# A transformer stack on one core: fp32 score products, another fill of the expert rows, other due times, and a place column for each tile

## The reference, cut to what matters

```python
# L0 xattn: causal-masked linear attention over the context; here Q is norm(x), K is ctx
x = x + _L0_xattn_ref(_layernorm(x), ctx)
# L0 ffn: inside it 16-head attention (head width 8) and 8 experts, top 2
...
scores = einsum('bhqd,bhkd->bhqk', q, k) / sqrt(8)      # q, k after rotary embedding
scores = where(causal, scores, -inf)
attn = softmax(scores)
x = x + (attn @ v) @ w_up
y_e = (silu(t @ w1[e]) * (t @ w3[e])) @ w2[e]            # 8 experts, width 512, the 2 best of a token
# L1 xattn: 16 heads of 64, queries from x, keys and values from the context
out = softmax(q @ k.T / 8) @ v @ w_out + b_out
# L1 ffn: 16 experts of width 256, the 2 best of a token, plus one shared expert of width 512
```

## Time and profile before

| what | us |
|---|---|
| median of 3 runs | 980.52 |
| lowest and highest run | 978.5, 985.04 |
| profiled execution, its own time | 989.18 |
| its span, first to last instruction | 987.4 |

### The profile page before, as it was taken

One profiled execution on the slowest core, in us unless ns is written; L12 is line 12 of the kernel. 1 busy time (PEld: TensorE's weight loads), 2 busy tenths in 40 slices (PEclk: granted clock), 3 DMA queues, 4 the chain that ended last, 5 costly groups with the idle time before them and its releaser, 6 DMA issues.

```text
span 987.4 us, 24585 instructions
## 1 busy us (share of the span) xinstructions
PE 910.0 (92%) x8304; PEld 813.8 (82%) x8304; DVE 723.1 (73%) x1957; ACT 611.7 (62%) x1694; POOL 293.6 (30%) x375
## 2 busy tenths in 40 slices
PE   4899889887999999998799999999998999898997
PEld 3776666654999999997699888998987988898896
DVE  5768788776676667674889978977876637776757
ACT  3487767773666666675577657786775236665640
POOL 3855666763000000001642435311212003232320
PEclk9899999998999999999799999999999999999999
DMA  8549999201131111113110132030028813232235
GB/s 293 160 161 300 352 245 253 56 29 55 53 137 55 49 51 53 55 34 117 43 35 12 33 98 76 23 98 23 23 65 352 290 44 87 77 90 85 82 114 190
DMA packets 59563, 109.82 MB, mean 111 GB/s; under 512 B 6225, under 2 KB 46033, under 8 KB 58033
## 3 DMA queue, kind: packets, MB, share of 16 engines
q1 hardware_dynamic: 52576, 89.42, 29.6%
q0 software_dynamic: 6864, 18.85, 5.7%
HBM read 62.24 MB, written 46.00 MB: 110 GB/s over the span
## 4 chain that ended last, share of the span: by engine, by line
PE 61%; issue 13%; DVE 9%; DMA 8%; POOL 5%; ACT 2%; SPq 0%; DVEq 0%; POOLq 0%; ACTq 0%
PE ps L888 15%; PE ps L718 8%; PE ps L720 8%; PE ps L719 8%; POOL yt_dram L1962 4%; PE ps L975 3%; DMA xs_dram<-zero 3%; PE ps L985 3%; PE ps L999 3%; PE ps L1057 2%; DMA kv_dram<-BIG 2%; PE ps L786 1%; PE ps L824 1%; PE ps L810 1%; ACT BIG L1151 1%
## 5 line engine op out<-in xcount | busy, mean ns | idle before, releaser
L718 PE MATMUL ps<-BIGR 128*128 128x256 f32 (+1 forms) x826 | 260.5, 315 | 6.5 <-DVE BIGR L1797 2.2
L888 PE MATMUL ps<-BIG 128*128 128x128 f32 x2000 | 253.8, 276 | 11.3 <-DVE BIG L1683 10.2
L888 PEld LDWEIGHTS ps<-BIG 128*128 128x128 f32 x2000 | 238.0, 192 | 15.4 <-DVE BIG L1683 13.1
L720 PE MATMUL ps<-BIGR 128*128 128x256 f32 x778 | 222.3, 286 | 0.0
L719 PE MATMUL ps<-BIGR 128*128 128x256 f32 (+1 forms) x602 | 179.2, 298 | 0.0
L718 PEld LDWEIGHTS ps<-BIGR 128*128 128x128 f32 x826 | 159.3, 193 | 14.4 <-issue 7.5
L720 PEld LDWEIGHTS ps<-BIGR 128*128 128x128 f32 x778 | 148.6, 191 | 0.7
L1197 ACT COPY BIG<-BIG 128x512 f32 (+1 forms) x86 | 70.1, 815 | 100.8 <-PE ps L888 87.2
L719 PEld LDWEIGHTS ps<-BIGR 128*128 128x128 f32 x602 | 116.3, 193 | 2.1 <-issue 0.3
L1676 DVE TENSOR_TENSOR BIGR<-BIG,BIGR 128x512 fp32r<-128x512 f32 (+1 forms) x86 | 80.3, 934 | 34.5 <-ACT BIGR L1206 34.3
L1954 POOL DMA_INDIRECT BIG<-ys_dram,YI x32 | 32.5, 1016 | 232.5 <-DMA ys_dram<-BIG 224.3
(11 more groups left out here) (234 smaller groups left out, 1916.5 us busy)
## 6 DMA issues: line engine op xcount, KB each, us to landing
xs_dram<-zero SPq DMA_DIRECT2D x17, 1024.0 KB, 19.5
BIG<-in_wgu SPq DMA_DIRECT2D x2, 6144.0 KB, 19.1
BIG<-in_wd SPq DMA_DIRECT2D x2, 4096.0 KB, 22.1
BIG<-xs_dram SPq DMA_DIRECT2D x47, 129.5 KB
BIG<-xs_dram SPq DMA_DIRECT2D x39, 128.0 KB
ys_dram<-BIG SPq DMA_DIRECT2D x39, 128.0 KB, 1.7
BIG<-in_wkv SPq DMA_DIRECT2D x2, 2048.0 KB, 9.9
kv_dram<-BIG SPq DMA_DIRECT2D x16, 256.0 KB, 4.1
```

The source lines that it names most:

```text
L718: pe.matmul(o, l[0], r[0], start=start, stop=False)
L720: return pe.matmul(o, l[1], r[0], start=False, stop=stop)
L888: i = pe.matmul(o[:, c * 128:(c + 1) * 128], wt[:, at:at + 128], x[:, k * 128:(k + 1) * 128], start=k == 0, stop=k == 1)
```

## The change

The scores of the first stage are computed from unrounded operands, in one product of fp32 for each row group and query half: queries 0 to 63 with all 128 keys of four heads (512 columns), queries 64 to 127 with keys 0 to 63 (256 columns) and with keys 64 to 127 (256 columns). The mask comes last and signals the banks. `qkl` and `kml` are gone. The rows of the first experts have a tensor of their own, `xs0_dram`, of 256 columns. It is filled by 16 DMAs in eight groups of two; each takes 1088 numbers in a run from every fourth partition of the context tile, so what fills the rows is context and not zeros (what is computed from a row that no token takes is never gathered). `IX` has a column for each tile, and `ix` no longer waits for a scatter. Waits on the loads of the first experts' rows in `pad_sp` and `sc` are gone. `LEAD` has other values.

```diff
-BLANK = [range(2 * g, 2 * g + 2) for g in range(7)] + [range(14, 17)]
+BLANK = [range(2 * g, 2 * g + 2) for g in range(8)]
 LEAD = {
-    "EC": -100, "ET": -200, "K": 100, "K_e": -700, "PV": -100, "Q_e": 200, "SD": 400, "V": 100, "V_e": -100,
-    "W": 100, "ah": -300, "al": -200, "btg": 1800, "c_e": -1700, "ch": 900, "cl": -700, "cnt": -100, "cpow": 1000,
-    "ctxh": -800, "ctxl": -1600, "ep1": -4200, "epow": -1400, "exp0": 200, "exp1": 300, "ga0": 4300,
-    "gates_a": -2300, "hnT": -300, "kmh": -100, "kvwl": -100, "kw": 600, "log": -100, "max3": -100, "nl": 200,
-    "ow": -300, "owl": 1200, "pT3": 100, "pT_e0": 400, "pow2": -1000, "pow3": 200, "pro1": 400, "pro2": -900,
-    "pv": -100, "qkT": -200, "qkv": -300, "qw": -200, "r": 100, "rope": -300, "rope_p": -100, "route1": 2400,
-    "sc1": 1100, "stats1": 800, "swh": 500, "swl": 600, "vw": 1100, "wx": 200, "xbt": 1300, "xf": -300, "xh": 700,
-    "xl": -3000, "xr": 1400
+    "EL": -200, "ET": -200, "K": 100, "K_e": -600, "PV": -300, "Q_e": 200, "SD": 400, "SG": 200, "V": 100,
+    "V_e": -200, "W": 100, "ah": -300, "al": -200, "btg": 2900, "c_e": -1600, "ch": 900, "cnt": -100, "cpow": 900,
+    "eps3": -300, "exp1": 200, "exp2": -200, "ga0": 4500, "gates_a": -6000, "hnT": -100, "hnT_e": -100, "kmh": -1200,
+    "kv_e": -600, "kvwl": -7500, "kwl": 800, "load_kv": 3200, "load_q": 2800, "max3": -300, "nl": 200, "owl": 1100,
+    "pT0": -100, "pT2": -500, "pT3": 100, "pT_e0": 200, "pT_e1": -100, "pT_e2": 100, "pow1": -3300, "pow2": -4500,
+    "pow3": 100, "pro1": 400, "pro2": -2800, "qkT": -600, "qkh": -100, "qkv": -1200, "qw": -700, "ra0": 200,
+    "ra1": -300, "rope": -400, "rope_p": -200, "sc0": 1600, "sc1": 1200, "sm": -800, "ss": 1600, "stats1": 300,
+    "swh": 300, "swl": 500, "tt": -2100, "vw": 1700, "wup": -300, "wx": 200, "xadd": -200, "xbt": 900, "xf": -200,
+    "xh": 1500, "xl": -1600, "xr": 600
 }
...
-        p.add("SP", 120, ("blank", g), ("tt", g - 1) if g else ("kmh", 0), late=4000)
+        p.add("SP", 120, ("blank", g), ("tt", 2 * g - 4) if g >= 2 else ("kmh", 2 * g), late=3000)
...
-        add("DVE", 340, ("qkl", b), ("qkh", b))
...
-        add("POOL", 1250, ("kml", b), ("qkl", b), ("s", b - 2))
-        add("PE", 1200, ("s", b), ("kmh", b), ("kml", b), banks=[("s", (f"exp{g}", b)) for g in range(4)])
+        add("PE", 1350, ("s", b), ("kmh", b), banks=[("s", (f"exp{g}", b)) for g in range(4)])
...
-            add("DVE", 100, "ix", ("xs", r, j), ("ys", r, j - 4), *([("te",)] if j == 0 else []))
+            add("DVE", 100, "ix", ("xs", r, j), *([("te",)] if j == 0 else []))
...
-                q, k = (qkh_[b % 2], qkl_[b % 2]), (kmh_[b % 2], kml_[b % 2])
-                for x, y in ((0, 0), (0, 1), (1, 0)):
-                    if y:
-                        causal(b)
-                        pe.wait_ge(*done("kml", b))
+                q, k = qkt_[b % 2], km_[b % 2].rearrange("p (n t) -> p n t", n=4)
+                for half, keys, masked_too in ((0, slice(0, 128), True), (1, slice(0, 64), False), (1, slice(64, 128), True)):
                     for g in range(4):
-                        at = slice(32 * g, 32 * g + 32)
-                        i = pe.matmul(ps("s", b, i=g)[:, :], q[x][at, 0:128], k[y][at, :], start=x + y == 0, stop=x == 1)
-                        if x == 1:
-                            i.then_inc(*fills("s", b, i=g))
+                        at, rows = slice(32 * g, 32 * g + 32), slice(64 * half, 64 * half + 64)
+                        o = ps("s", b, i=g)[rows, :].rearrange("p (n t) -> p n t", n=4)
+                        pe.matmul(o[:, :, keys], q[at, rows], k[at, :, keys], start=True, stop=not masked_too)
+                causal(b)
...
+                    for rows in range(2):
+                        last[rows].then_inc(*fills("s", b, i=2 * (rows ^ 1) + n))
...
-                if j >= 4:
-                    v.wait_ge(sem(f"results_placed{(j - 4) % 3}"), 16 * stores_before(1, j - 4))
...
             def blank(g):
 
-                if g:
-                    sp.wait_ge(*done("tt", g - 1))
-                    if g >= 3:
-                        sp.wait_ge(sem(f"cleared{g % 3}"), 16 * sum(len(BLANK[k]) for k in range(g % 3, g, 3)))
+                if g == 0:
+                    sp.wait_ge(sem("ct_loaded1"), 16 * (NB // 2 - 2 - len(EARLY_KV)))
+                    sp.wait_ge(sem("ct_loaded2"), 16 * len(EARLY_KV))
+                    sp.wait_ge(*done("kmh", 0))
+                elif g == 1:
+                    sp.wait_ge(*done("kmh", 2))
                 else:
-                    sp.wait_ge(*done("kmh", 0))
-                    sp.wait_ge(sem("zeroed"), 1)
+                    sp.wait_ge(*done("tt", 2 * g - 4))
+                if g >= 3:
+                    sp.wait_ge(sem(f"cleared{g % 3}"), 16 * sum(len(BLANK[k]) for k in range(g % 3, g, 3)))
                 for c in BLANK[g]:
-                    sp.dma_start(XS[0:E0 * CAP, 0:D].rearrange("(e c) n -> c e n", c=CAP)[128 * c:128 * c + 128],
-                                 zero[:, 0:D].rearrange("p (o n) -> p o n", o=1).broadcast_to([128, E0, D])
+                    n = CAP // 16 * D // 32
+                    sp.dma_start(XS0.rearrange("r n -> (r n)").rearrange("(e s k n) -> s k e n", e=E0, s=16, k=32)[c],
+                                 CT[c % 4:128:4, :, :, :].rearrange("p b k t -> p (b k t)")[:, 0:n]
+                                 .rearrange("p (o n) -> p o n", o=1).broadcast_to([32, E0, n])
                                  ).then_inc(sem(f"cleared{g % 3}"), 16)
```

More of the change, by code:

```diff
@@ L502, in program @@
         freed = [sem(f"freed{i}") for i in range(8)]
+        XS0 = nc.dram_tensor("xs0_dram", [E0 * CAP, D], F32, kind="Internal").ap()
         XS = nc.dram_tensor("xs_dram", [E1 * CAP, ROW], F32, kind="Internal").ap()
@@ L598, in program @@
         lat = Space((104, 116))
-        qkh_ = lat.ring(2, 256, r=True)
-        qkl_ = lat.ring(2, 256, r=True)
-        kmh_ = lat.ring(2, 512, r=True)
-        kml_ = lat.ring(2, 512, r=True)
+        qkt_ = lat.ring(2, 256)
+        km_ = lat.ring(2, 512)
         lat = Space((96, 104), (116, 152))
@@ L795, in causal @@
                 for n in range(2):
+                    last = [None, None]
                     for half in range(2):
@@ L801, in causal @@
                             o = ps("s", b, i=g)[64 * half:64 * half + 64, :].rearrange("p (n t) -> p n t", n=4)[:, :, lo:128]
-                            pe.matmul(o, identb[at, at], m.broadcast_to([64, 4, 128 - lo]), start=False, stop=False)
+                            last[rows] = pe.matmul(o, identb[at, at], m.broadcast_to([64, 4, 128 - lo]), start=False, stop=True)
+                    for rows in range(2):
+                        last[rows].then_inc(*fills("s", b, i=2 * (rows ^ 1) + n))
             def pT(b, g):
@@ L1141, in qkh @@
                     act.wait_ge(*full("s", b - 2, i=3))
-                act.copy(qkh_[b % 2], ps("qkT", b)[:, 0:256]).then_inc(S["qk_hi"], 1)
+                act.copy(qkt_[b % 2], ps("qkT", b)[:, 0:256]).then_inc(*frees("qkT", b))
             def exp(b, g):
@@ L1631, in ix @@
                 then()
-                v.scalar_tensor_tensor(out=IX[:, j % 4:j % 4 + 1], in0=xs[:, D + 2:ROW], scalar=128.0 * j,
+                v.scalar_tensor_tensor(out=IX[:, j:j + 1], in0=xs[:, D + 2:ROW], scalar=128.0 * j,
                                        in1=PL[:, j % 4:j % 4 + 1], op0=ALU.mult,
@@ L1904, in kmh @@
             def kmh(b):
-                pool.wait_ge(*done("qkh", b))
+                pool.wait_ge(*emptied("qkT", b))
                 if b >= 2:
                     pool.wait_ge(*full("s", b - 2, i=3))
-                masked(pool, kmh_[b % 2], qkh_[b % 2][:, 128:256]).then_inc(S["keys_masked_hi"], 1)
+                masked(pool, km_[b % 2], qkt_[b % 2][:, 128:256]).then_inc(S["keys_masked"], 1)
             def kvwl(u):
@@ L1915, in kvwl @@
                                    ALU.subtract).then_inc(S["early_w_lo"], 1)
-            def kml(b):
-                pool.wait_ge(*emptied("qkT", b))
-                if b >= 2:
-                    pool.wait_ge(*full("s", b - 2, i=3))
-                masked(pool, kml_[b % 2], qkl_[b % 2][:, 128:256]).then_inc(S["keys_masked_lo"], 1)
             def xr(b):
@@ L1936, in sc @@
                             pool.wait_ge(sem(f"cleared{g % 3}"), 16 * sum(len(BLANK[k]) for k in range(g % 3, g + 1, 3)))
-                if r and b == 0:
-                    for i in range(3):
-                        pool.wait_ge(sem(f"rows_loaded{i}"), 16 * len(range(i, NT0, 3)))
                 for k in range(2):
-                    pool.indirect_dma_start(XS, bass.IndirectOffsetOnAxis(ap=PI[:, b, k:k + 1], axis=0),
-                                            TT[tile_of(r, b)][:, :], None).then_inc(sem(f"scattered{tile_of(r, b)}"), 16)
+                    pool.indirect_dma_start(XS if r else XS0, bass.IndirectOffsetOnAxis(ap=PI[:, b, k:k + 1], axis=0),
```

(5 more changed lines are left out.)

19 lines of the change are left out of this document (7 added, 12 removed).

## The result

| | before | after |
|---|---|---|
| median of 4 runs each | 982.78 us | 943.81 us |
| lowest and highest | 978.5, 986.55 | 939.74, 946.33 |
| profiled execution, its span | 987.4 us | 941.6 us |

The ratio is 0.9601, 95% interval 0.9544 to 0.9657: 39 us faster, where 18.4 were forecast. In three later series, on chips A, C and D, the same kernel gained less (0.972 to 0.979, 963 to 968 us, while the kernel before took 987 to 989); the last experiments are about that. Every ratio leaves out the runs in the chip's slower state, such as one of e13's ten (1275 us, at a granted clock of 0.656).

A forecast was written before the change was run, and what follows sets the result against it. TensorE was taken as the bound, its matmul queue busy 910.0 of 987.4 us. First stage -4.5, seam -4.9 and second experts -9.0 made -18.4: 970.8 us profiled, 962.1 for the median; range 946 to 979.

The forecast's parts named there:

- all idle time goes: Rival: idle time goes in first stage, seam and second experts, -31 us in all, 949.5 us; chance 0.06.
- The sum: Whole kernel: first stage -4.5, seam -4.9, second experts -9.0, together -18.4 us.
- Part 1, the products: First stage's scores: products and mask take 1.95 us a batch, +0.30 each, +4.8 us of TensorE work.
- The like row: Scores' mask: 2 x (512 + 256) columns of each row half in 0.55 us, showing one row group's tiles can overlap.
- the end that I had priced at -3: Scores: query halves overlap wholly, 1.47 us a batch, -0.18 each, -3 us over 16.
- The first stage's sum: First stage: half of 18.6 us idle time goes, -9.3; with +4.8 of work, -4.5; bounds -22 and +12.
- the store's wait: First stage: ScalarE waited 4.1 us for a key and value store behind two old fill DMAs; this should go.
- Part 2, the fill: First experts' rows: 16 spread DMAs take 41 to 71 us of transfer; waits of 10.3 us should go.
- The GpSimd wait: First stage: GpSimd waited 6.2 us for the old fill in two scatters; no such wait should remain.
- the share: Sign for the fill: a DMA share under 0.7 between 120 and 170 us.
- Part 3, the seam: Before cross attention: last expert store goes before two weight loads, gather 5 us earlier, -4.9 us; bounds 0 and -8.
- Part 4, the places: Second experts: VectorE's place wait goes, TensorE-bound, a tile every 2.9 us, -9.0 us; bounds -9.2 and 0.

The follow-up runs named there:

- e13: The changed kernel with two due times (`kvwl`, `kv_e`) set back to the old order, against the kernel before; 987.05 us, ratio 1.0007, chip C.
- e6: The changed kernel with all the old due times put back, against the kernel before; 990.48 us, ratio 1.003, chip B.
- e2: The kernel before with the new fill of the first experts' rows alone; 985.04 us, ratio 0.9986, chip A.
- e1: The kernel before with the new fp32 scores alone; 999.27 us, ratio 1.0121, chip A.
- e15: The changed kernel, unaltered, measured again beside the kernel before; 962.91 us, ratio 0.9764, chip C.
- e3: The kernel before with a place column for each tile alone; 975.56 us, ratio 0.9875, chip A.
- e11: The kernel before with the new due time of `load_q` (2800) alone; 989.05 us, ratio 0.9984, chip A.
- e9: The changed kernel, unaltered, measured again beside the kernel before; 963.48 us, ratio 0.9723, chip A.
- e5: The changed kernel with the old fill put back, against the kernel before; 970.26 us, ratio 0.9834, chip B.
- e8: The changed kernel with both query halves in one 512-column product per row group, against the kernel before; 968.0 us, ratio 0.9812, chip B.

## Why the prediction was wrong in size

The direction held. The time fell out of the range by 2 us, at the side of "all idle time goes" (949.5), but not as that rival says: 8.3 us of idle time are left between 60 and 205 us, and most of the miss is busy time. The sum had -18.4 us, made of 23.2 less idle and 4.8 more busy time; the profiled executions differ by 45.8, made of 31.7 less idle and 14.1 less busy time. Of the 27.4 us between them 15.4 lie in the first stage and 9.9 in the last two windows (by the work that moved, 11 in the second experts and -1 at the seam). The other 2.1 lie in the first experts, where nothing was forecast: they take 208.2 us in every kernel with the new due times and 209.9 to 210.3 in every one with the old. The medians differ by less, and the miss there is 18 us, because the profiled execution of before was 8.7 us above the median that the forecast started from (980.52) and that of after is at its own.

On chips A, C and D the ratio is 0.972 to 0.979, near the forecast's 0.981. That is partly luck: on chip A the first stage gained 6 us where 4.5 was the sum of a wrong +4.8 and a -9.3 that was too much there.

**Part 1, the products: wrong.** The step was: "a product is two instructions in program order, so the second half's first product can start only when the first half's second instruction has started". All eight start within 0.05 us. The like row, the mask's overlap, was at hand and was outvoted by an argument. Forecast +4.8 us, measured 16 x (1.60 - 1.65) = -0.8, near the end that I had priced at -3. The 512 columns of two halves took 1.05 us up to the mask, where 0.92 was worked out from the earlier trace rows, a form of other shape. The difference, 0.13, is an estimate of what the one change of tiling mode before the mask can cost at most; 0.19 was read from the earlier trace rows. The Trainium skill ("TensorEngine Tiling (Array Packing)", section "Tiling Modes") says that such a change drains TensorE. No run here shows the drain by itself.

**The first stage's sum: wrong.** The step was "I take half of it: -9.3": that the relief of work and of the fill would give half of the stage's short waits back in whatever order. It was no reading of a mechanism. With scores, fill and places new and the old due times the stage gives nothing back: it is longer than before (e6: 258.1; the whole 1.003). I had priced the store's wait at 4.1 us, from the earlier trace rows, as a wait of the old fill. Only about half of it was: with the new fill and all else old 2.0 us of it stay (e2). The rest is a wait of the order. With the new scores in the old order it grows to 14 us and TensorE's clock falls with it (e1, e6), and two due times decide whether it comes (e13 against e15). I treated the due times as a seam of 5 us and nothing else in the stage. On record the idle time fell by 16.3 us and the busy time by 3.6, of which the products are 0.8; on chip A the idle time fell by 6 (41.7 and 42.1 us in e3 and e11, 35.5 in e9) and the busy time not at all (204.8 and 204.0, then 204.4). So what the runs show is that the gain hangs on the stores; how large it is without the pauses stays open, and 13 of the record's 19.9 us were not seen again.

**Part 2, the fill: right in the rows, small in worth.** The GpSimd wait went, the share fell to 0.30, the transfers spread; at 279 GB/s they move near the slow end of the forecast (250). Alone it is worth nothing measurable (e2), in company some 2 us, no more than the noise (e5 against e8).

**Part 3, the seam: right.** -4.9 forecast, 8.4 to 3.9 us measured. TensorE's wait there (L1019) is still 3.0 us of the 4.9. From the gather to the second experts 340.9 us became 337.9, but 3.6 us of work moved out of this window, so cross attention gained nothing, as forecast.

**Part 4, the places: right in mechanism, mis-sized.** -9.0 forecast from idle time between 810 and 932 alone; measured -16.4 on record, 20 with the moved work, and -16 alone (e3). The idle part over the whole stretch was 12.1. The rest is busy time: I had taken it as work and set a tile at 2.9 us; it came at 2.74.

## What to carry to other kernels

Before costing a part of a change by what it removes, look which transfers stand in front of which in SyncE's queue: a store that frees a buffer must not stand behind a load that nobody needs soon, and when the compute ahead of it gets shorter the same order can cost more (here 4 us became 14). Where an engine's runs are broken by waits, its busy time is not its work; take the cost of a step from a stretch without waits. Parts which act on one stage are to be run in company, not one by one. Windows of two traces are only as comparable as their work: count the instructions in both.

## What the runs showed of the hardware

- fp32 products of 32 rows into both halves of the array's columns run side by side although each is two instructions: 512 and 512 columns in 1.05 us, the same as one 128-wide product (1.07).
- While a fill in runs of 4,352 bytes from 32 partitions went on, the core moved 279 GB/s; with 1 KB pieces from 128 partitions, 250. The time from issue to landing (7.3 and 19.5 us) is for the most part what stands in the queue: the first 1 MB of the 1 KB pieces landed in 6.2.
- In this program TensorE pauses 0.5 to 0.7 us in its densest run of instructions (some 80 to 98 instructions in) in the traces of chips A to D and not in the one on record; a product of 0.77 us placed in a run that pauses takes the pause's place.
